# A recurrence of 1024 steps: bf16 splits of three gate products against float32 products with constant matmuls beside them

## The chip, the cores and the metric

The kernel runs as one program on 1 core of a Trainium2 chip. The metric is the device time of one execution in microseconds (us); lower is better. A core has five engines with instruction streams of their own: TensorE (PE in the rows, its weight loads PEld), VectorE (DVE), ScalarE (ACT), GpSimd (POOL) and SyncE (SP). [...] 

## The reference, cut to what matters

The program is a small network: six transformer layers, a gated recurrence over the sequence, six more layers, an expert layer, full attention and a second expert layer, with layer norms between. Only the recurrence is touched by the change. Its input is `x` with B = 2 rows of T = 1024 steps and 128 features; the state has 128 features.

```python
def step(carry, inp):
    h, c, n = carry
    xi_t, xf_t, xg_t, xo_t = inp            # x @ W*x + b, known ahead
    i_t = jax.nn.sigmoid(xi_t + h @ Wih)
    f_t = jax.nn.sigmoid(xf_t + h @ Wfh)
    g_t = jnp.tanh(xg_t + h @ Wgh)
    o_t = jax.nn.sigmoid(xo_t + h @ Woh)
    c_t = f_t * c + i_t * g_t
    n_t = f_t * n + i_t * jnp.exp(g_t @ Weg + beg)
    h_t = o_t * (c_t / n_t)
    return ((h_t, c_t, n_t), h_t)
```

Each step needs the `h` of the step before, so the 1024 steps are a chain.

## The kernel before, in words

Everything runs with features on the 128 partitions; a state is 128x2 (two rows of the batch). `recurrence_phase` (lines 952 to 1161) first loads the weights, splits those of the gates i, f and o into three bf16 parts each (lines 1004 to 1010), and then loops over 8 rounds (`Fori`, line 1078) of `ROUND` = 128 unrolled steps. A round is made of 8 chunks of `CH` = 16 steps; the chunks alternate between two sets of PSUM banks (`j`) and two buffers `hbuf`. The parts of a gate that don't depend on `h` (bias and `x @ W`) are put into the banks one chunk ahead by `project`, as 9 pieces: a float32 product of 32 columns after each odd step (line 1065), one more after step 0 (line 1067). The products with `h` are added on top of these.

The order of each engine is written out by hand, with a semaphore for each hand-over. In one step:

- TensorE (`tensor_steps`, lines 1048 to 1061): waits for `h_ready`; float32 product of gate g, which the compiler issues as two weight loads and two matmuls; then, from the three bf16 parts of `h` and of the weights, six small matmuls for each of i and f (a weight load each) and six for o; then it waits for `tg_ready` and does the float32 product with `Weg`; then a piece of `project` where one is due.
- ScalarE (lines 1089 to 1099): tanh of g, exp of -(i, f) together, exp of -o, exp of the `Weg` product.
- VectorE (lines 1109 to 1149): sigmoids from the exponentials, then the new denominator times (1 + e^-o) as `no`, the new numerator `cn[0]`, `rn = 1/no`, `h = cn[0] * rn` into `hbuf`; after that it makes the three bf16 parts of `h` (`hparts`, lines 1138 to 1143) and the new `cn[1]` (line 1146), off the way to `h`. A `scalar_tensor_tensor` whose scalar is a column per partition is issued once for each of the two batch rows.
- GpSimd adds `x` to a chunk of 16 `h` (line 1156) once that chunk is complete.

A wait that matters, in the code:

```python
                if n:
                    pe.wait_ge(h_ready, n)
                pe.matmul(g_bank[j][:, s * B:(s + 1) * B], Wg[:, 3, 1, :], h, start=False, stop=True,
                          skip_group_check=True).then_inc(g_done, 1)
```

The pieces of `project` and all else that follows on TensorE stand behind this wait in program order, and the next step's product stands behind them.

Of the kernel before, what the change touches and what calls it, by code (L numbers as in the profile page):

```python
# [933 lines left out]
GATES = ("i", "f", "o", "g")  # L941

EARLY_TERMS = [(0, 0), (1, 0), (2, 0), (0, 1), (1, 1)]
LAST_TERM = (0, 2)

MOST = 1e37


def recurrence_phase(nc, c):

    with ExitStack() as ctx:
        sb, ps, sem = scope(nc, ctx)  # L960
        Wg = sb("Wgates", [P, 4, 2, P])
        Wparts = sb("Wparts", [P, 3, 3, P], BF16)
        wrest = sb("wrest", [P, 3, P])
# [8 lines left out]
        g_bank = [ps(f"g_bank{i}", [P, 512]) for i in range(2)]
        s_bank = [ps(f"s_bank{i}", [P, 512]) for i in range(2)]
        o_bank = [ps(f"o_bank{i}", [P, 512]) for i in range(2)]
        e_bank = [ps(f"e_bank{i}", [P, 512]) for i in range(2)]
        w_in, zeroed, w_split, table_loaded = sem("r_w_in"), sem("r_zeroed"), sem("r_w_split"), sem("r_table_loaded")
        counted = [sem("r_" + x) for x in (
            "g_done", "s_done", "o_done", "e_done", "tg_ready", "es_ready", "ex_ready", "eo_ready", "h_ready",
            "h_first", "h_split", "rest_done", "so_done", "nso_done", "sg_done", "fno_done", "ig_done", "n_done", "no_done", "rn_done", "y_done")]
        (g_done, s_done, o_done, e_done, tg_ready, es_ready, ex_ready, eo_ready, h_ready,  # L980
         h_first, h_split, rest_done, so_done, nso_done, sg_done, fno_done, ig_done, n_done, no_done, rn_done, y_done) = counted

        with nc.Block() as block:
# [9 lines left out]
            @block.gpsimd  # L993
            def _(pool):
                pool.memset(cn[:, :, :], 0.0).then_inc(zeroed, 1)
                pool.memset(hbuf[1][:, :, :], 0.0).then_inc(zeroed, 1)
                pool.memset(hparts[:, :, :], 0.0).then_inc(zeroed, 1)

            @block.vector
            def _(dve):  # L1000

                dve.wait_ge(w_in, 16 * 10)
                W = Wg[:, 0:3, 1, :]
                dve.tensor_copy(Wparts[:, :, 0, :], W).then_inc(w_split, 1)
                dve.wait_ge(w_split, 1)
                dve.tensor_tensor(wrest[:, :, :], W, Wparts[:, :, 0, :], ALU.subtract).then_inc(w_split, 1)
                dve.wait_ge(w_split, 2)
                dve.tensor_copy(Wparts[:, :, 1, :], wrest[:, :, :]).then_inc(w_split, 1)
                dve.wait_ge(w_split, 3)
                dve.tensor_tensor(Wparts[:, :, 2, :], wrest[:, :, :], Wparts[:, :, 1, :], ALU.subtract).then_inc(w_split, 1)  # L1010

        def tensor_steps(pe, it, first_round):
            def project(j, at, which):


                gate, part = which // 2, which % 2
                if gate != 0 and gate != 1:
                    bank = {2: o_bank, 3: g_bank, 4: e_bank}[gate]
                    out = bank[j][:, 0:CH * B].rearrange("p (s b) -> p b s", b=B)
                    first = part == 0  # L1020
                else:
                    out = s_bank[j][:, 0:CH * 2 * B].rearrange("p (s g b) -> p g b s", g=2, b=B)[:, gate]
                    first = which == 0
                if part == 0:
                    lhsT, rhs = bias[0:1, gate, :], c.ones[0:1, 0:B * CH].rearrange("p (b s) -> p b s", b=B)
                else:
                    lhsT, rhs = Wg[:, gate, 0, :], c.xA[:, :, bass.ds(at, CH)]
                return pe.matmul(out, lhsT, rhs, start=first, stop=False, skip_group_check=True)

            def recur(out, gate, terms):  # L1030
                for w_part, h_part in terms:
                    last = pe.matmul(out, Wparts[:, gate, w_part, :], hparts[:, h_part, :], start=False,  # L1032
                                     stop=(w_part, h_part) == LAST_TERM, skip_group_check=True)
                return last
# [43 lines left out]
        with nc.Fori(0, T // ROUND) as it:  # L1078
            with nc.Block() as block:
# [5 lines left out]
                def _(act):  # L1085
                    for n in range(ROUND):
                        k, s = divmod(n, CH)
                        j = k % 2
                        act.wait_ge(g_done, n + 1)
                        act.activation(tg[:, :], g_bank[j][:, s * B:(s + 1) * B], ACT.Tanh).then_inc(tg_ready, 1)  # L1090
                        act.wait_ge(s_done, n + 1)
                        act.activation(es[:, :, :].rearrange("p g b -> p (g b)"), s_bank[j][:, s * 2 * B:(s + 1) * 2 * B],  # L1092
                                       ACT.Exp, scale=-1.0).then_inc(es_ready, 1)
                        act.wait_ge(o_done, n + 1)
                        act.activation(eo[:, :], o_bank[j][:, s * B:(s + 1) * B], ACT.Exp, scale=-1.0).then_inc(eo_ready, 1)
                        if n:
                            act.wait_ge(n_done, n)
                        act.wait_ge(e_done, n + 1)
                        act.activation(ex[:, :], e_bank[j][:, s * B:(s + 1) * B], ACT.Exp).then_inc(ex_ready, 1)

                @block.vector
                def _(dve):

                    for n in range(ROUND):
                        k, s = divmod(n, CH)
                        j = k % 2
                        if s == 0 and k >= 2:
                            dve.wait_ge(y_done, k - 1)
                        dve.wait_ge(es_ready, n + 1)
                        dve.tensor_scalar(sg[:, :, :], es[:, :, :], 1.0, None, ALU.add).then_inc(sg_done, 1)  # L1110
                        dve.wait_ge(eo_ready, n + 1)
                        dve.tensor_scalar(so[:, :], eo[:, :], MOST, 1.0, ALU.min, ALU.add).then_inc(so_done, 1)
                        dve.wait_ge(sg_done, 2 * n + 1)
                        dve.reciprocal(sg[:, :, :], sg[:, :, :]).then_inc(sg_done, 1)
                        dve.wait_ge(so_done, n + 1)
                        dve.tensor_tensor(nso[:, :], cn[:, 1, :], so[:, :], ALU.mult).then_inc(nso_done, 1)
                        dve.wait_ge(sg_done, 2 * n + 2)
                        dve.tensor_tensor(iso[:, :], sg[:, 0, :], so[:, :], ALU.mult)
                        dve.wait_ge(nso_done, n + 1)
# [499 lines left out]
```

## Time and profile before

| what | value |
|---|---|
| time, median of 3 runs | 7952.26 us |
| runs, lowest to highest | 7947.48 to 7956.73 us |
| span of the profiled execution, first to last instruction | 7947.7 us |
| stretch with the 1024 steps in it | 2336 to 5190 us of the span |
| mean granted TensorE clock over the span | 0.795 of full speed |

The span is the profiled execution itself; no other time is listed for it, and the three timed runs lie between 0.2 us below it and 9.0 us above it. The rows are read so: a row of the timeline gives the start, then the duration of the instructions on it from the first one's start to the last one's end (`x12` is 12 of them, which overlap), then in brackets the idle time of the engine before it and what ended that. [...]

### The profile page before, as it was taken

How to read it: one execution, taken by the hardware profiler on the slowest of the kernel's cores; microseconds unless marked ns; L12 is line 12 of the kernel's file. 1: busy time of each engine (PE TensorE's matmuls, PEld its weight loads, DVE VectorE, ACT ScalarE, POOL GpSimd, SP SyncE). 2: the span in 40 equal slices, each digit the busy share in tenths (PEclk: the TensorE clock that was granted, in tenths of full speed). 3: DMA queues.
4: the chain of work that ended last, by engine and by line, in shares of the span. 5: the costliest groups of instructions: out<-in, count | busy, mean ns of one | idle time of the engine just before them, and what ended most of it. 6: DMA issues, size and time to landing. Idle time of an engine off the chain costs nothing. (4 is left out here: it accounts for less than half of the span.)

```text
span 7947.7 us, 238408 instructions
## 1 busy us (share of the span) xinstructions
PE 6508.3 (82%) x89716; PEld 4710.8 (59%) x89716; DVE 5680.7 (71%) x26551; ACT 2813.2 (35%) x7328; POOL 1991.7 (25%) x2075
## 2 busy tenths in 40 slices
PE   8999999999976666666666666679999999999887
PEld 5656656565656565655656565656565655656544
DVE  6676767676767777777777777777666676767566
ACT  4444444444432222222222222234444444444311
POOL 4343535353510000000000000034444353535200
PEclk9999999999975555555555555589999999999898
DMA  0000000000000000000000000000000000000000
GB/s 28 11 4 14 1 14 1 14 1 14 1 15 2 2 2 2 2 2 2 2 2 2 2 2 2 2 4 0 15 11 4 11 4 14 1 14 1 18 2 12
DMA packets 30765, 50.49 MB, mean 6 GB/s; under 512 B 2032, under 2 KB 25291, under 8 KB 28235
## 3 DMA queue, kind: packets, MB, share of 16 engines
q1 hardware_dynamic: 29614, 40.54, 1.6%
q8 instruction: 425, 6.96, 0.4%
q14 instruction: 314, 2.56, 0.1%
q10 hardware_dynamic: 412, 0.42, 0.0%
HBM read 39.91 MB, written 1.05 MB: 5 GB/s over the span
## 5 line engine op out<-in xcount | busy, mean ns | idle before, releaser
L1048 PE MATMUL g_bank<-hbuf,Wgates 128*128 128x2 f32 x2048 | 600.9, 363 | 1024.2 <-DVE hbuf L1136 970.3
L1048 PEld LDWEIGHTS g_bank<-hbuf,Wgates 128*128 128x128 f32 x2048 | 513.0, 311 | 1140.0 <-DVE hbuf L1136 1085.3
L1090 ACT ACTIVATE tg<-g_bank 128x2 f32<-128x2 f32 x1024 | 176.1, 172 | 1690.9 <-PE g_bank L1048 1690.9
L1156 POOL TENSOR_TENSOR xB<-hbuf,xA 128x32 f32 x64 | 16.4, 256 | 2853.0 <-DVE hbuf L1136 2853.0
L371 POOL TENSOR_TENSOR t1b<-t1b,t2b 128x1024 f32<-128x1024 f32 x192 | 451.7, 2354 | 687.1 <-DVE t2b L523 687.1
L371 POOL TENSOR_TENSOR t1a<-t1a,t2a 128x1024 f32<-128x1024 f32 x192 | 451.7, 2354 | 684.7 <-DVE t2a L523 684.7
L1060 PE MATMUL e_bank<-tg,Weg 128*128 128x2 f32 x2048 | 579.4, 352 | 0.0
L1032 PEld LDWEIGHTS s_bank<-hparts,Wparts 128*128 128x128 bf16 x12288 | 571.0, 117 | 0.0
L1110 DVE TENSOR_SCALAR sg<-es 128x4 f32<-128x4 f32 x1024 | 174.4, 170 | 554.5 <-ACT es L1092 554.5
L1060 PEld LDWEIGHTS e_bank<-tg,Weg 128*128 128x128 f32 x2048 | 515.1, 312 | 0.0
L1032 PE MATMUL s_bank<-hparts,Wparts 128*128 128x2 bf16 x12288 | 469.6, 165 | 0.0
L555 DVE TENSOR_REDUCE ssqb<-sqb 128x16 f32<-128x1024 f32 x192 | 232.7, 1215 | 187.5 <-ACT sqb L634 187.5
L376 POOL TENSOR_TENSOR t1b<-t1b,rnormb 128x1024 f32<-128x1024 f32 x192 | 361.1, 1902 | 11.6 <-DVE rnormb L98 11.6
L376 POOL TENSOR_TENSOR t1a<-t1a,rnorma 128x1024 f32<-128x1024 f32 x192 | 361.0, 1901 | 11.6 <-DVE rnorma L98 11.6
L555 DVE TENSOR_REDUCE ssqa<-sqa 128x16 f32<-128x1024 f32 x192 | 232.5, 1215 | 182.3 <-ACT sqa L634 182.3
L1127 DVE SCALAR_TENSOR_TENSOR no<-ex,iso,fno 128x1 f32<-128x1 f32 x2048 | 352.0, 213 | 3.6 <-issue 1.7
L1146 DVE SCALAR_TENSOR_TENSOR cn<-ex,sg,fcn 128x1 f32<-128x1 f32 x2048 | 351.8, 214 | 0.0
L431 PEld LDWEIGHTS banksa<-KT,QTa 64*32 64x32 f32 x12288 | 292.1, 107 | 41.0 <-issue 41.0
L431 PEld LDWEIGHTS banksb<-KT,QTb 64*32 64x32 f32 x12288 | 292.1, 107 | 40.7 <-issue 40.7
L643 ACT COPY Vwb<-banksb 128x512 f32<-128x512 f32 x384 | 224.8, 586 | 256.5 <-PE banksb L475 256.1
L643 ACT COPY Vwa<-banksa 128x512 f32<-128x512 f32 x384 | 224.7, 586 | 255.9 <-PE banksa L475 255.5
L431 PE MATMUL banksa<-KT,QTa 64*32 64x64 f32 x12288 | 308.3, 218 | 0.0
(435 smaller groups left out, 16401.7 us busy)
## 6 DMA issues: line engine op xcount, KB each, us to landing
Wqkv<-in_L_ffn_Wqkv SPq DMA_DIRECT2D x13, 1536.0 KB, 6.5
Wo<-in_L_ffn_Wo SPq DMA_DIRECT2D x13, 512.0 KB, 7.6
W<-in_L_ffn_W SPq DMA_DIRECT2D x12, 341.0 KB
W<-in_L_ffn_W SPq DMA_DIRECT2D x12, 128.0 KB
xt<-in_L_attn_x SPq DMA_DIRECT2D x2, 512.0 KB
rope<-in_rope SPq DMA_DIRECT2D x1, 1024.0 KB, 7.5
out<-ot SPq DMA_DIRECT2D x4, 256.0 KB
W<-in_L_ffn_W SPq DMA_DIRECT2D x12, 42.5 KB
```

Of the source, the lines that this page charges most:

```text
L371: pool.tensor_tensor(t1[:, part], t1[:, part], t2[:, part], ALU.add).then_inc(s.rot_sum, 1)
L376: pool.tensor_tensor(qview(t1[:, part]), qview(t1[:, part]), c.rnorm[:, i * HEADS:(i + 1) * HEADS].unsqueeze(2).to_broadcast([P, HEADS, DH ...
L431: last = pe.matmul(sc[WIN * w:WIN * w + WIN, col:col + KEYS], c.QT[rows, pair, WIN * w:WIN * w + WIN], c.KT[b][rows, pair, WIN * w:WIN * w ...
L555: dve.tensor_reduce(c.ssq[:, i * HEADS:(i + 1) * HEADS], qview(sq[:, i * INNER:(i + 1) * INNER]), AX.X, ALU.add).then_inc(s.ssq_done, 1)
L643: act.copy(c.Vw[:, w, :], vo[:, bank * 512:(bank + 1) * 512]).then_inc(s.v_ready, 1)
L1032: last = pe.matmul(out, Wparts[:, gate, w_part, :], hparts[:, h_part, :], start=False, stop=(w_part, h_part) == LAST_TERM, skip_group_chec ...
L1048: pe.matmul(g_bank[j][:, s * B:(s + 1) * B], Wg[:, 3, 1, :], h, start=False, stop=True, skip_group_check=True).then_inc(g_done, 1)
L1060: pe.matmul(e_bank[j][:, s * B:(s + 1) * B], Weg[:, :], tg[:, :], start=False, stop=True, skip_group_check=True).then_inc(e_done, 1)
L1090: act.activation(tg[:, :], g_bank[j][:, s * B:(s + 1) * B], ACT.Tanh).then_inc(tg_ready, 1)
L1110: dve.tensor_scalar(sg[:, :, :], es[:, :, :], 1.0, None, ALU.add).then_inc(sg_done, 1)
L1127: last = dve.scalar_tensor_tensor(out=no[:, b:b + 1], in0=ex[:, b:b + 1], scalar=iso[:, b:b + 1], in1=fno[:, b:b + 1], op0=ALU.mult, op1=A ...
L1146: last = dve.scalar_tensor_tensor(out=cn[:, 1, b:b + 1], in0=ex[:, b:b + 1], scalar=sg[:, 0, b:b + 1], in1=fcn[:, 1, b:b + 1], op0=ALU.mul ...
```

## The change

All gate weights stay float32: the split of the weights, `hparts`, `hrest` and the four instructions that made them in each step go. The step on TensorE is now float32 products of i, g and f, the wait for the tanh, the `Weg` product, the float32 product of o, then `project` where due, and then `warm` = 4 matmuls after even steps and 3 after odd ones, with constant bf16 operands (the identity as weights, 512 columns of the mask), into a PSUM bank that nobody reads. ScalarE has five activations instead of four (i and f apart). VectorE keeps numerator and denominator over the common denominator f: `w = (1+e^-f)/(1+e^-i)`, `up = cn + w * (tanh g, exp)`, `h = up[0] / (up[1] * (1+e^-o))`, `cn = up / (1+e^-f)`. The order of the nine pieces of `project` and the placing of gates in banks change with it. Cut to its core (`...` marks what is left out):

```diff
-EARLY_TERMS = [(0, 0), (1, 0), (2, 0), (0, 1), (1, 1)]
-LAST_TERM = (0, 2)
-MOST = 1e37
+MOST = 1e30
-def recurrence_phase(nc, c):
+def recurrence_phase(nc, c, warm=4):
...
+        spare = ps("spare_bank", [P, 512])
...
-                dve.tensor_copy(Wparts[:, :, 0, :], W).then_inc(w_split, 1)
...
         def tensor_steps(pe, it, first_round):
+            pieces = [("e", 4, 0), ("i", 0, 0), ("i", 0, 1), ("f", 1, 0), ("f", 1, 1), ("o", 2, 0), ("o", 2, 1), ("g", 3, 0), ("g", 3, 1)]
...
+            def recur(gate, row, j, s, h):
+                return pe.matmul(columns(gate, j, s), Wg[:, row, 1, :], h, start=False, stop=True, skip_group_check=True)
...
                 if n:
                     pe.wait_ge(h_ready, n)
-                pe.matmul(g_bank[j][:, s * B:(s + 1) * B], Wg[:, 3, 1, :], h, start=False, stop=True,
-                          skip_group_check=True).then_inc(g_done, 1)
-                if n:
-                    pe.wait_ge(h_split, 2 * n - 1)
-                recur(i_out, 0, EARLY_TERMS)
-                recur(f_out, 1, EARLY_TERMS)
-                if n:
-                    pe.wait_ge(h_split, 2 * n)
-                recur(i_out, 0, [LAST_TERM])
-                recur(f_out, 1, [LAST_TERM]).then_inc(s_done, 1)
-                recur(o_out, 2, EARLY_TERMS + [LAST_TERM]).then_inc(o_done, 1)
+                recur("i", 0, j, s, h).then_inc(i_done, 1)
+                recur("g", 3, j, s, h).then_inc(g_done, 1)
+                recur("f", 1, j, s, h).then_inc(f_done, 1)
                 pe.wait_ge(tg_ready, n + 1)
-                pe.matmul(e_bank[j][:, s * B:(s + 1) * B], Weg[:, :], tg[:, :], start=False, stop=True,
-                          skip_group_check=True).then_inc(e_done, 1)
+                pe.matmul(columns("e", j, s), Weg[:, :], tg[:, :], start=False, stop=True, skip_group_check=True).then_inc(e_done, 1)
+                recur("o", 2, j, s, h).then_inc(o_done, 1)
+                if s == 0:
+                    project(1 - j, 0, 0)
                 if s % 2 == 1:
-                    project(1 - j, it * ROUND + (PAD + (k + 1) * CH), s // 2)
-                if s == 0:
-                    project(1 - j, 0, 8)
+                    project(1 - j, it * ROUND + (PAD + (k + 1) * CH), 1 + s // 2)
+                for _ in range(warm if s % 2 == 0 else max(warm - 1, 0)):
+                    pe.matmul(spare[:, :], c.identb[:, :], c.mask[:, :, :].rearrange("p t j -> p (t j)"), start=True, stop=True)
...
+                        act.wait_ge(i_done, n + 1)
+                        act.activation(ei[:, :], columns("i", j, s), ACT.Exp, scale=-1.0).then_inc(ei_ready, 1)
                         act.wait_ge(g_done, n + 1)
+                        act.activation(tg[:, :], columns("g", j, s), ACT.Tanh).then_inc(tg_ready, 1)
+                        act.wait_ge(f_done, n + 1)
+                        act.activation(ef[:, :], columns("f", j, s), ACT.Exp, scale=-1.0).then_inc(ef_ready, 1)
+                        act.wait_ge(e_done, n + 1)
+                        act.activation(ex[:, :], columns("e", j, s), ACT.Exp).then_inc(ex_ready, 1)
                         act.wait_ge(o_done, n + 1)
+                        act.activation(eo[:, :], columns("o", j, s), ACT.Exp, scale=-1.0).then_inc(eo_ready, 1)
...
+                        dve.wait_ge(ei_ready, n + 1)
+                        dve.tensor_scalar(di[:, :], ei[:, :], 1.0, None, ALU.add).then_inc(di_done, 1)
+                        dve.wait_ge(di_done, n + 1)
+                        dve.reciprocal(ri[:, :], di[:, :]).then_inc(ri_done, 1)
+                        dve.wait_ge(ef_ready, n + 1)
+                        dve.tensor_scalar(df[:, :], ef[:, :], MOST, 1.0, ALU.min, ALU.add).then_inc(df_done, 1)
+                        dve.wait_ge(ri_done, n + 1)
+                        dve.wait_ge(df_done, n + 1)
+                        dve.tensor_tensor(w[:, :], df[:, :], ri[:, :], ALU.mult).then_inc(w_done, 1)
+                        dve.reciprocal(rf[:, :], df[:, :]).then_inc(rf_done, 1)
+                        dve.wait_ge(w_done, n + 1)
+                        for b in range(B):
+                            last = dve.scalar_tensor_tensor(out=up[:, 0, b:b + 1], in0=tg[:, b:b + 1], scalar=w[:, b:b + 1],
+                                                            in1=cn[:, 0, b:b + 1], op0=ALU.mult, op1=ALU.add)
+                        last.then_inc(c_done, 1)
+                        dve.wait_ge(ex_ready, n + 1)
+                        for b in range(B):
+                            last = dve.scalar_tensor_tensor(out=up[:, 1, b:b + 1], in0=ex[:, b:b + 1], scalar=w[:, b:b + 1],
+                                                            in1=cn[:, 1, b:b + 1], op0=ALU.mult, op1=ALU.add)
+                        last.then_inc(n_done, 1)
+                        dve.wait_ge(eo_ready, n + 1)
+                        dve.wait_ge(n_done, n + 1)
+                        dve.scalar_tensor_tensor(out=mo[:, :], in0=eo[:, :], scalar=1.0, in1=up[:, 1, :],
+                                                 op0=ALU.add, op1=ALU.mult).then_inc(mo_done, 1)
+                        dve.wait_ge(mo_done, n + 1)
+                        dve.reciprocal(rm[:, :], mo[:, :]).then_inc(rm_done, 1)
...
+                        dve.wait_ge(rm_done, n + 1)
+                        dve.tensor_tensor(hbuf[j][:, :, s], up[:, 0, :], rm[:, :], ALU.mult).then_inc(h_ready, 1)
+                        dve.wait_ge(rf_done, n + 1)
+                        dve.tensor_tensor(cn[:, :, :], up[:, :, :], rf[:, :].unsqueeze(1).to_broadcast([P, 2, B]), ALU.mult).then_inc(state_done, 1)
+                        dve.wait_ge(state_done, n + 1)
```

## Rows read from the trace of the kernel before

**Rows 1.** The page: busy time by engine, and granted clock in 40 slices.

```profile
PE 6508.3 (82%) x89716; PEld 4710.8 (59%) x89716; DVE 5680.7 (71%) x26551; ACT 2813.2 (35%) x7328; POOL 1991.7 (25%) x2075
...
PEclk9999999999975555555555555589999999999898
```

**Rows 2.** Who waited for whom from 2336 to 5190: total us, times, longest.

```profile
PEld g_bank L1048 <- DVE hbuf L1136: 1085.3, 1016, 1.6
DVE sg L1110 <- ACT es L1092: 547.4, 1023, 7.7
PEld g_bank L1048 <- issue: 54.1, 7, 8.2
```

**Rows 3.** The timeline from 3000 to 3006, all engines: one step of it.

```profile
3000.83 0.16 DVE L1136 TENSOR_TENSOR hbuf<-cn,rn 128x2 f32<-128x2 f32 x1
...
3001.05 0.50 PEld L1048 LDWEIGHTS g_bank<-hbuf,Wgates 128*128 128x128 f32 x2 [0.83 <-DVE hbuf L1136]
3001.05 0.58 PE L1048 MATMUL g_bank<-hbuf,Wgates 128*128 128x2 f32 x2 [0.69 <-DVE hbuf L1136]
...
3001.49 0.46 PE L1032 MATMUL s_bank<-hparts,Wparts 128*128 128x2 bf16 x12
3001.67 0.17 ACT L1090 ACTIVATE tg<-g_bank 128x2 f32<-128x2 f32 x1 [1.61 <-PE g_bank L1048]
...
3001.95 0.50 PEld L1060 LDWEIGHTS e_bank<-tg,Weg 128*128 128x128 f32 x2
3001.97 0.57 PE L1060 MATMUL e_bank<-tg,Weg 128*128 128x2 f32 x2
3001.99 0.17 ACT L1092 ACTIVATE es<-s_bank 128x4 f32<-128x4 f32 x1
...
3002.27 0.17 DVE L1110 TENSOR_SCALAR sg<-es 128x4 f32<-128x4 f32 x1 [0.48 <-ACT es L1092]
...
3002.47 0.50 PEld L1028 LDWEIGHTS s_bank<-ones,gate_bias 1*128 1x128 f32 x2
3002.47 0.18 DVE L1114 RECIPROCAL sg<-sg 128x4 f32<-128x4 f32 x1
...
3002.97 0.34 DVE L1127 SCALAR_TENSOR_TENSOR no<-ex,iso,fno 128x1 f32<-128x1 f32 x2
3003.23 0.16 DVE L1131 TENSOR_TENSOR cn<-ig,fcn 128x2 f32<-128x2 f32 x1
3003.35 0.17 DVE L1133 RECIPROCAL rn<-no 128x2 f32<-128x2 f32 x1
3003.55 0.16 DVE L1136 TENSOR_TENSOR hbuf<-cn,rn 128x2 f32<-128x2 f32 x1
...
3003.77 0.50 PEld L1048 LDWEIGHTS g_bank<-hbuf,Wgates 128*128 128x128 f32 x2 [0.80 <-DVE hbuf L1136]
```

**Rows 4.** The timeline: weight loads of an expert's 512-column float32 matmuls.

```profile
7549.98 0.33 PEld L1312 LDWEIGHTS ezmoe<-Wemoe,ext0moe 128*128 128x128 f32 x1 [0.52 <-issue]
7550.83 0.33 PEld L1312 LDWEIGHTS ezmoe<-Wemoe,ext0moe 128*128 128x128 f32 x1 [0.52 <-issue]
```

**Rows 5.** Busy time by stretch: from:to, us, engines, PEclk, DMA share, GB/s.

```profile
2312.50:2319.30 6.80, 4.46 (x16) 2.86 (x16) 4.91 (x16) 2.35 (x4) 0.00 (x0) 0.50 0.00 0
2327.70:2333.30 5.60, 5.11 (x18) 4.48 (x18) 0.00 (x0) 1.49 (x2) 0.00 (x0) 0.50 0.00 0
2336.00:5190.00 2854.00, 1829.23 (x23656) 1708.35 (x23656) 2193.18 (x19444) 692.29 (x4092) 16.38 (x64) 0.50 0.01 2
7548.96:7551.68 2.72, 2.72 (x3) 1.17 (x4) 0.53 (x3) 0.00 (x0) 0.18 (x1) 0.50 0.00 0
7552.20:7555.60 3.40, 3.40 (x9) 1.52 (x8) 3.24 (x14) 0.00 (x0) 0.29 (x1) 1.00 0.03 7
7807.90:7811.30 3.40, 3.08 (x12) 2.15 (x12) 2.50 (x8) 1.64 (x3) 0.00 (x0) 0.50 0.00 0
```

**Rows 6.** Groups of 7528.6 to 7530.9: 20-column float32 matmuls at clock 1.00.

```profile
L1214 PE MATMUL elmoe<-wg2moe,hTmoe 32*128 32x20 f32 x20 | 2.4, 262 | 0.0
```

More of the change, by code:

```diff
@@ L972, in recurrence_phase @@
[L972 to L976, printed above, removed]
+        tg, ei, ef, eo, ex = sb("tg", [P, B]), sb("ei", [P, B]), sb("ef", [P, B]), sb("eo", [P, B]), sb("ex", [P, B])
+        di, ri, df, rf, w = sb("di", [P, B]), sb("ri", [P, B]), sb("df", [P, B]), sb("rf", [P, B]), sb("w", [P, B])
@@ L977, in recurrence_phase @@
+        cn, up = sb("cn", [P, 2, B]), sb("up", [P, 2, B])
+        mo, rm = sb("mo", [P, B]), sb("rm", [P, B])
+        io_bank = [ps(f"io_bank{i}", [P, 512]) for i in range(2)]
+        ge_bank = [ps(f"ge_bank{i}", [P, 512]) for i in range(2)]
+        f_bank = [ps(f"f_bank{i}", [P, 512]) for i in range(2)]
+        spare = ps("spare_bank", [P, 512])
+        w_in, zeroed, table_loaded = sem("r_w_in"), sem("r_zeroed"), sem("r_table_loaded")
         counted = [sem("r_" + x) for x in (
-            "g_done", "s_done", "o_done", "e_done", "tg_ready", "es_ready", "ex_ready", "eo_ready", "h_ready",
@@ L983, in recurrence_phase @@
+        (i_done, g_done, f_done, e_done, o_done, ei_ready, tg_ready, ef_ready, ex_ready, eo_ready,
+         h_ready, di_done, ri_done, df_done, w_done, c_done, n_done, mo_done, rm_done, rf_done, state_done, y_done) = counted
         with nc.Block() as block:
@@ L996, in _, with columns @@
                 pool.memset(hbuf[1][:, :, :], 0.0).then_inc(zeroed, 1)
[L997 to L1003, printed above, removed]
-                dve.tensor_copy(Wparts[:, :, 0, :], W).then_inc(w_split, 1)
[L1005 to L1010, printed above, removed]
+        def columns(gate, j, s, width=1):
+            bank, at = {"i": (io_bank, 0), "o": (io_bank, 1), "g": (ge_bank, 0), "e": (ge_bank, 1), "f": (f_bank, 0)}[gate]
+            at = (at * CH + s) * B
+            return bank[j][:, at:at + width * B]
@@ L1012, in tensor_steps @@
         def tensor_steps(pe, it, first_round):
+            pieces = [("e", 4, 0), ("i", 0, 0), ("i", 0, 1), ("f", 1, 0), ("f", 1, 1), ("o", 2, 0), ("o", 2, 1), ("g", 3, 0), ("g", 3, 1)]
             def project(j, at, which):
[L1016 to L1020, printed above, removed]
-                else:
-                    out = s_bank[j][:, 0:CH * 2 * B].rearrange("p (s g b) -> p g b s", g=2, b=B)[:, gate]
-                    first = which == 0
@@ L1024, in project @@
[L1024 to L1034, printed above, removed]
+                gate, row, part = pieces[which]
@@ new lines, in project @@
+                out = columns(gate, j, 0, CH).rearrange("p (s b) -> p b s", b=B)
+                if part == 0:
+                    lhsT, rhs = bias[0:1, row, :], c.ones[0:1, 0:B * CH].rearrange("p (b s) -> p b s", b=B)
+                else:
+                    lhsT, rhs = Wg[:, row, 0, :], c.xA[:, :, bass.ds(at, CH)]
+                return pe.matmul(out, lhsT, rhs, start=(gate in ("e", "i", "f") and part == 0), stop=False, skip_group_check=True)
+            def recur(gate, row, j, s, h):
+                return pe.matmul(columns(gate, j, s), Wg[:, row, 1, :], h, start=False, stop=True, skip_group_check=True)
@@ L1111, in _ @@
[L1111 to L1117, printed above, removed]
@@ L1125, in _ @@
-                        dve.wait_ge(ex_ready, n + 1)
-                        for b in range(B):
-                            last = dve.scalar_tensor_tensor(out=no[:, b:b + 1], in0=ex[:, b:b + 1], scalar=iso[:, b:b + 1],
-                                                            in1=fno[:, b:b + 1], op0=ALU.mult, op1=ALU.add)
-                        last.then_inc(no_done, 1)
-                        dve.wait_ge(ig_done, n + 1)
-                        dve.tensor_tensor(cn[:, 0, :], ig[:, :], fcn[:, 0, :], ALU.add)
@@ L1132, in _ @@
-                        dve.wait_ge(no_done, n + 1)
-                        dve.reciprocal(rn[:, :], no[:, :]).then_inc(rn_done, 1)
-                        dve.wait_ge(rn_done, n + 1)
-                        h = hbuf[j][:, :, s]
-                        dve.tensor_tensor(h, cn[:, 0, :], rn[:, :], ALU.mult).then_inc(h_ready, 1)
-                        dve.tensor_tensor(hparts[:, 0, :], cn[:, 0, :], rn[:, :], ALU.mult).then_inc(h_first, 1)
-                        dve.wait_ge(h_first, n + 1)
@@ L1140, in _ @@
-                        dve.tensor_tensor(hparts[:, 1, :], h, hparts[:, 0, :], ALU.subtract).then_inc(h_split, 1)
-                        dve.tensor_tensor(hrest[:, :], h, hparts[:, 0, :], ALU.subtract).then_inc(rest_done, 1)
-                        dve.wait_ge(rest_done, n + 1)
-                        dve.tensor_tensor(hparts[:, 2, :], hrest[:, :], hparts[:, 1, :], ALU.subtract).then_inc(h_split, 1)
-                        for b in range(B):
-                            last = dve.scalar_tensor_tensor(out=cn[:, 1, b:b + 1], in0=ex[:, b:b + 1], scalar=sg[:, 0, b:b + 1],
-                                                            in1=fcn[:, 1, b:b + 1], op0=ALU.mult, op1=ALU.add)
@@ L1148, in _ @@
-                        last.then_inc(n_done, 1)
-                        dve.wait_ge(n_done, n + 1)
+                        dve.wait_ge(c_done, n + 1)
+                        dve.wait_ge(rm_done, n + 1)
+                        dve.tensor_tensor(hbuf[j][:, :, s], up[:, 0, :], rm[:, :], ALU.mult).then_inc(h_ready, 1)
+                        dve.wait_ge(rf_done, n + 1)
+                        dve.tensor_tensor(cn[:, :, :], up[:, :, :], rf[:, :].unsqueeze(1).to_broadcast([P, 2, B]), ALU.mult).then_inc(state_done, 1)
```

31 lines of the change are left out of this document (2 added, 29 removed).

## The prediction

> **What bounds the kernel now.** I read the page first: TensorE is busy 82% of the span, but its granted clock is at half for the whole middle of it, 2336 to 5190 [rows 1]. In that stretch no engine is full: TensorE 1829 of 2854 us, VectorE 2193 [rows 5]. That is the picture of a chain, and the waits say which: TensorE waits 1085 us for `h`, VectorE 547 us for the exponentials [rows 2]. The timeline of a step then gives the chain piece by piece. From `h` to `h` (3000.83 to 3003.55) it takes 2.72 us [rows 3]: 0.22 to the first weight load; 0.58 for the float32 product of g; 18 small bf16 matmuls from 3001.49 to 3001.97, 0.027 each; the exponential at 3001.99; 0.28 to VectorE; 1.28 there until `h` is written again. 1024 steps at 2.72 are 2785 us of the 2854; the other 69 (0.07 a step) are mostly the starts of the 8 rounds (TensorE "issue" 54 us in 7 pieces [rows 2]). I keep the 69.
>
> So the change is worth 1024 times what it does to a step. The sum is made against the span of the profiled execution, 7947.7 us; the median of the runs is 4.6 us above, and I put the result on the median.
>
> [...] Removed: 18 bf16 matmuls, 0.48 us. Added: float32 products of i, f and o. A float32 product costs two weight loads. Where the next weights can be loaded behind it, the next matmul starts 0.44 after it (g at 3001.05, first bf16 matmul at 3001.49); from the `Weg` product to the next product's load it is 0.52 (3001.95 to 3002.47) [rows 3]. i, g, f, e and o follow each other like the first case, so 5 x 0.445 = 2.23; bound 5 x 0.52 = 2.60. Does e wait for the tanh? g ends at 0.445 + 0.58 = 1.03; the tanh starts 0.04 later, takes 0.17, and TensorE answers 0.05 after: 1.29, before f gives up its place at 1.34. No stall. `project` is 9 products in 16 steps, of 0.5: 0.28 a step.
>
> The constant matmuls are 3.5 a step, 512 columns each. Their form in bf16 isn't timed here at this clock; the nearest rows are the expert's float32 matmuls, 0.85 us from one weight load to the next at 7550 [rows 4] (clock 0.50 there [rows 5]), which at the full clock are 8 loads in 3.40 us, 0.425 each [rows 5]. [...] 3.5 x 0.43 = 1.50. One thing comes back: the first weight load of the next step's i hides under the last constant matmul, -0.21.
>
> Sum: 2.23 + 0.28 + 1.50 - 0.21 = **3.80 us of TensorE per step**; bound above 4.2 (products at 0.52, constant ones at 0.45), below 3.70.
>
> [...] Times from the first load of i, dependent VectorE instructions 0.20 apart (3002.27 to 3002.47, 3003.35 to 3003.55), a pair of `scalar_tensor_tensor` 0.26 until the next instruction and 0.38 until one that needs it (3002.97 to 3003.35) [rows 3]. f ends at 0.89 + 0.58 = 1.47; exp 1.51 to 1.68; `df` 1.79; `w` 1.99; first pair 2.19; second pair 2.45 (exp of e at 1.96 to 2.13, in time); `mo` 2.83; `rm` 3.04; `h` 3.24; next load 3.46. The o path (o ends 2.36, exp until 2.57) isn't last. So 3.46 of chain against 3.80 of TensorE: the constant matmuls are **not** in a gap, they stand in front of the next i and set the step. Without them it would already be slower than 2.72, as three products at half clock take 1.3 where 18 small matmuls took 0.48. That `w` and the pair over the common denominator come only after f, and `hparts` falls away, is inside this sum; the `hparts` instructions were off the path already (the load of g doesn't wait for them). What goes before the loop (four conversions) happens once. GpSimd's addition follows `h` as before and covers itself. ACT has 5 x 0.17 = 0.85 of work in 3.8. None of these adds to the sum.
>
> **Total at 1.2 GHz:** 1024 x 3.82 (0.02 for hand-over) = 3912, plus 69 = 3981 for the stage against 2854: +1127. 7947.7 + 1127 = 9075, with the 4.6 of the median 9079; I say **9075 us**. Bounds: step 3.70: 8957; step 4.2: 9469.
>
> **Which clock.** All hangs on this. The stage is entered at 0.50 and the rows show what TensorE did without a rise: 64% busy with small products for 2854 us; 91% busy (5.11 of 5.60) with float32 products of 32 columns at 2327.7; 16 transposes of 128 columns in 6.80 us (their columns pass for 16 x 0.213 = 3.4 us, half the time) at 2312.5; even 12 of them in 3.40 us at 7807.9, also at 0.50 [rows 5]. The rise shown is after 512-column matmuls stood end to end for 2.7 us (7548.96 to 7551.68, then 1.00) [rows 5]. In a step of 3.8 us at half clock the constant matmuls pass columns for 1.5 us in one block, 1.3 or 1.7 us long, 39% of the time; between blocks stand products of 2 columns, the kind that never raised anything. This resembles the stretch at 2312.5 and not the one at 7549. So I take 0.50 throughout.
>
> [...]
>
> **Rivals.**
>
> 1. *The full clock comes and holds.* A product of few columns then costs 20 instructions in 2.3 us, 0.115 x 2 = 0.23, and ends 0.115 + 0.26 = 0.38 after its first load [rows 6]. i 0, g 0.23, f 0.46, ending 0.38, 0.61, 0.84. ScalarE: exp i, tanh 0.65 to 0.82, exp f 0.88 to 1.05. `df` 1.16, `w` 1.36, pairs 1.56 and 1.82, `mo` 2.20, `rm` 2.41, `h` 2.61, load 2.83. TensorE needs 5 x 0.23 + 0.14 + 3.5 x 0.215 = 2.04 and is hidden. Step 2.82 against 2.72: +102 us, **8055**. Even then VectorE's longer tail has eaten the faster products. [...] Against it: the stretches above, and that such a step leaves TensorE waiting 0.8 us with narrow work beside.
> 2. *The other side: full clock and a shorter tail.* Place: f to `w` to the two pairs. If the o path ended last, not this one, `mo` would start at 1.82 (o ends 0.88 + 0.23 + 0.38 = 1.49, exp to 1.71) and the step take 2.45; halfway is 2.6: 1024 x -0.12 = -123, **7829**. It decides in the kernel's favour as soon as the step is under 2.72. Against it: it needs both the clock and dependent instructions closer than 0.20 everywhere, which no row shows.
> 3. *The clock changes back and forth*, some steps at 3.8, some at 2.8: **8100 to 8950**. For it: blocks of wide columns sometimes lie near each other. Against it: at half clock each is followed by 2.0 us of narrow products, so nothing starts the first rise.
> 4. *The constant matmuls are left out or cost nothing*: the chain alone, 3.46: 7952 + 1024 x 0.74 = **8710**. Nothing in the diff lets them go; the bank is written and never read, but they are instructions.
>
> **How the numbers follow.** Forecast 0.80, its own range 8955 to 9430, as 9469 needs every product at 0.52. Rival 1 0.07, rival 2 0.05, its neighbour within 0.2% of no change 0.01, rivals 3 and 4 together 0.07. The forecast's own range holds about 0.77 (what it misses lies mostly just below, where products overlap more); down to 8700 come rival 4 and a part of 3: 0.80. So the range is 8700 to 9430. 0.2%, some 16 us, is about what a measurement of this kernel can tell from no change. Faster 0.06, same 0.02, slower 0.92.
>
> **What would show it.** Right: granted clock 0.50 over the whole recurrence, which is 3.9 to 4.1 ms long; TensorE over 95% busy in it; waits of TensorE for `h` almost gone; constant matmuls 0.43 apart; the row of `h` 3.8 us apart; VectorE idle over 1 us a step. Wrong: PEclk of 1.00 anywhere inside the stage (rivals 1 to 3); steps of 2.8 with `h` as TensorE's releaser (1); steps of 3.8 whose i waits for `h` (then my chain is too short, not my TensorE too long); products 0.52 apart would put it at 9.3 to 9.4 ms.

## The result and the profile after

| | before | after |
|---|---|---|
| median | 7949.87 us | 8999.45 us |
| ratio after/before, 95% interval | | 1.1315 (1.1297 to 1.1333) |
| span of the profiled execution | 7947.7 us | 8997.6 us |
| mean granted clock of the span | 0.795 | 0.76 |
| first `h` to last `h` | 2853.0 us | 3895.0 us |

One of the four runs of the changed kernel took 12406 us with a mean clock of 0.52; it is left out of the ratio (without it the median is 8999.32 us), and nothing below rests on it.

The kernel is 1050 us slower, 1042 of them between the first and the last `h`. The page of the kernel after, to be read against [rows 1] (PEclk is the granted clock, the share of its full speed that TensorE's clock had, here in tenths):

```profile
PE 8529.1 (95%) x81012; PEld 5970.6 (66%) x81012; DVE 5402.8 (60%) x20403; ACT 3000.2 (33%) x8352; POOL 1990.8 (22%) x2074
...
PEclk9999999999655555555555555555999999999988
```

TensorE went from 82% to 95% busy with fewer instructions, and the clock's valley is as deep as before and wider. Two stretches of it, against [rows 5]; the columns are those of that group:

```profile
2341.00:6233.00 3892.00, 3849.37 (x14951) 2965.37 (x14952) 1916.58 (x13294) 879.22 (x5112) 15.26 (x63) 0.50 0.00 1
4000.00:4100.00 100.00, 100.00 (x391) 77.13 (x392) 50.19 (x348) 23.22 (x135) 0.24 (x1) 0.50 0.00 1
```

TensorE is busy for 3849 of 3892 us, 100 of 100 in the middle, and its granted clock stays at 0.50. Who waited for whom in this stretch, against [rows 2]:

```profile
DVE di L1058 <- ACT ei L1041: 1143.4, 1022, 7.6
...
DVE df L1062 <- ACT ef L1045: 416.9, 1014, 0.5
PEld io_bank L995 <- DVE hbuf L1087: 384.2, 952, 0.8
...
PE io_bank L995 <- issue: 42.6, 7, 6.3
```

Before, both TensorE (1085 us) and VectorE (547 us) waited. Now TensorE's matmuls wait for `h` nowhere; a weight load does for 384 us, behind a constant matmul that is still running. VectorE waits 1143 + 417 us. One step of the kernel after, one without a piece of `project`, against [rows 3] (the first row is from the step before):

```profile
3999.83 0.56 PE L995 MATMUL ge_bank<-hbuf,Wgates 128*128 128x2 f32 x2
...
4002.71 0.16 DVE L1087 TENSOR_TENSOR hbuf<-up,rm 128x2 f32<-128x2 f32 x1
...
4002.99 0.76 PEld L995 LDWEIGHTS io_bank<-hbuf,Wgates 128*128 128x128 f32 x2 [0.28 <-DVE hbuf L1087]
4003.42 0.43 PE L995 MATMUL io_bank<-hbuf,Wgates 128*128 128x2 f32 x2
...
4003.71 0.56 PE L995 MATMUL ge_bank<-hbuf,Wgates 128*128 128x2 f32 x2
...
4004.13 0.57 PE L995 MATMUL f_bank<-hbuf,Wgates 128*128 128x2 f32 x2
...
4004.56 0.57 PE L1011 MATMUL ge_bank<-tg,Weg 128*128 128x2 f32 x2
...
4004.94 0.17 DVE L1062 TENSOR_SCALAR df<-ef 128x2 f32<-128x2 f32 x1 [0.41 <-ACT ef L1045]
4004.99 0.56 PE L995 MATMUL io_bank<-hbuf,Wgates 128*128 128x2 f32 x2
...
4005.21 0.16 DVE L1065 TENSOR_TENSOR w<-df,ri 128x2 f32<-128x2 f32 x1
...
4005.41 1.87 PE L1018 MATMUL spare_bank<-mask,identb 128*128 128x512 bf16 x4
...
4006.13 0.16 DVE L1079 SCALAR_TENSOR_TENSOR mo<-eo,up 128x2 f32<-128x2 f32 x1
...
4006.33 0.17 DVE L1082 RECIPROCAL rm<-mo 128x2 f32<-128x2 f32 x1
4006.60 0.16 DVE L1087 TENSOR_TENSOR hbuf<-up,rm 128x2 f32<-128x2 f32 x1
...
4006.82 0.59 PEld L995 LDWEIGHTS io_bank<-hbuf,Wgates 128*128 128x128 f32 x2 [0.44 <-DVE hbuf L1087]
4007.07 0.42 PE L995 MATMUL io_bank<-hbuf,Wgates 128*128 128x2 f32 x2
```

This is a queue and not a chain. From i to the next i, 3.65 us: 0.29 for i (its first weight load is hidden), then 0.42, 0.43, 0.43, 0.42 for the other four products, then four constant matmuls until 4007.07, 0.415 each. `h` has been there since 4006.76. The step before has a piece of `project` and one constant matmul less, and takes 3.88 (its g product at 3999.83, this one's at 4003.71). The chain through VectorE is close behind: without the constant matmuls a step takes 3.55 us (`e1_none` below), 0.10 less than this one.

### The profile page after: what moved, and what is told of

It is laid out like the page before. It is cut to its first block and busy times, and to the rows that moved or that the text cites. A ratio compares the mean times of both kernels' runs of the same rounds, so it can differ in the third digit from the quotient of the medians.

```text
span 8997.6 us, 216915 instructions
## 1 busy us (share of the span) xinstructions
PE 8529.1 (95%) x81012; PEld 5970.6 (66%) x81012; DVE 5402.8 (60%) x20403; ACT 3000.2 (33%) x8352; POOL 1990.8 (22%) x2074
## 5 line engine op out<-in xcount | busy, mean ns | idle before, releaser
L1018 PE MATMUL spare_bank<-mask,identb 128*128 128x512 bf16 x3584 | 1706.9, 624 | 0.0
L995 PEld LDWEIGHTS io_bank<-hbuf,Wgates 128*128 128x128 f32 x4096 | 1196.2, 326 | 478.8 <-DVE hbuf L1087 384.2
L995 PE MATMUL io_bank<-hbuf,Wgates 128*128 128x2 f32 x4096 | 1021.1, 319 | 43.2 <-issue 42.6
L1018 PEld LDWEIGHTS spare_bank<-mask,identb 128*128 128x128 bf16 x3584 | 503.6, 164 | 444.2 <-issue 423.7
L995 PE MATMUL ge_bank<-hbuf,Wgates 128*128 128x2 f32 x2048 | 579.5, 353 | 0.0
L1011 PE MATMUL ge_bank<-tg,Weg 128*128 128x2 f32 x2048 | 579.5, 353 | 0.0
L995 PE MATMUL f_bank<-hbuf,Wgates 128*128 128x2 f32 x2048 | 579.5, 353 | 0.0
L995 PEld LDWEIGHTS ge_bank<-hbuf,Wgates 128*128 128x128 f32 x2048 | 559.7, 333 | 0.0
L995 PEld LDWEIGHTS f_bank<-hbuf,Wgates 128*128 128x128 f32 x2048 | 559.7, 333 | 0.0
L1011 PEld LDWEIGHTS ge_bank<-tg,Weg 128*128 128x128 f32 x2048 | 517.9, 313 | 0.0
```

The costliest lines, as they stand in the source:

```text
L995: return pe.matmul(columns(gate, j, s), Wg[:, row, 1, :], h, start=False, stop=True, skip_group_check=True)
L1011: pe.matmul(columns("e", j, s), Weg[:, :], tg[:, :], start=False, stop=True, skip_group_check=True).then_inc(e_done, 1)
L1018: pe.matmul(spare[:, :], c.identb[:, :], c.mask[:, :, :].rearrange("p t j -> p (t j)"), start=True, stop=True)
```

## The experiments

Each run stands beside runs of the kernel before on the same chip, medians of which were 7947 to 7953 us.

### Four runs that take the change apart

`e1_none` is the changed kernel without the constant matmuls (first diff), `e2_eight` with twice as many (`warm=8` in the same line), `e3_burst` keeps its 4 and puts a burst of 20 ahead of each round (second diff), and `e4_update` puts the new update alone into the kernel before (third diff: TensorE, ScalarE and the parts of `h` stay as before).

```diff
-def recurrence_phase(nc, c, warm=4):
+def recurrence_phase(nc, c, warm=0):
```

```diff
+            for _ in range(20):
+                pe.matmul(spare[:, :], c.identb[:, :], c.mask[:, :, :].rearrange("p t j -> p (t j)"), start=True, stop=True)
             for n in range(ROUND):
```

```diff
+                        dve.tensor_scalar(di[:, :], es[:, 0, :], 1.0, None, ALU.add).then_inc(di_done, 1)
+                        dve.tensor_scalar(df[:, :], es[:, 1, :], MOST, 1.0, ALU.min, ALU.add).then_inc(df_done, 1)
...
-                        dve.tensor_scalar(sg[:, :, :], es[:, :, :], 1.0, None, ALU.add).then_inc(sg_done, 1)
...
-                        dve.tensor_tensor(h, cn[:, 0, :], rn[:, :], ALU.mult).then_inc(h_ready, 1)
...
+                        dve.tensor_tensor(h, up[:, 0, :], rm[:, :], ALU.mult).then_inc(h_ready, 1)
```

> The changed kernel with no constant matmuls (warm = 0), all else the same. Theory 1 (TensorE's own work sets the step, the constant matmuls stand in front of the next i product): what is left is the chain i, g, f, exp of f, df, w, two pairs, mo, rm, h. With the distances of the changed kernel's trace (mo to rm 0.19, rm to h 0.27, h to the next load 0.22) a step is 3.4 to 3.55 us instead of 3.74: total 8700 to 8830 us, clock still 0.50. Theory 2 (the chain through VectorE is already last and the constant matmuls are hidden): about 9000 us. Theory 3 (they do help the clock somewhere): over 9000 us.

> The changed kernel with 8 constant matmuls after even steps and 7 after odd ones. Theory 1 (the clock rises when wide matmuls fill enough of what TensorE does; 4 a step were too few): the block of 3.4 us at half clock lifts it, PEclk 1.00 in the recurrence, a float32 product then takes 0.22, a constant matmul 0.215, and TensorE's sum 1.1 + 0.14 + 1.6 meets the chain of about 2.8: step 2.8 to 3.0, total 8050 to 8250 us. Theory 2 (nothing with narrow products between the blocks lifts it): step 2.0 + 0.3 + 7.5 x 0.43 - 0.2 = 5.3 us, total 10500 to 10700 us, PEclk 0.50.

> The changed kernel with 20 extra constant matmuls back to back at the start of each of the 8 rounds (8.5 us at half clock, about 6 with the rise in it), which should lift the clock once a round. Theory 1 (4 a step neither lift nor hold it): PEclk 1.00 for some us after each burst, then 0.50 again; total 9010 to 9070 us. Theory 2 (4 a step are enough to hold a clock that is up, they only could not raise it): PEclk 1.00 through the round, step about 2.85, total 8050 to 8200 us.

> The kernel before with its bf16 products, and only VectorE's update over the common denominator taken from the change. Theory 1 (the longer tail on VectorE is a cost of its own, hidden in the changed kernel by TensorE): from the exponentials at 0.94 the chain di, ri, w, two pairs, mo, rm, h ends 3.1 to 3.3 us after the load of g instead of 2.72: total 8300 to 8550 us. Theory 2 (all of the loss is the float32 products and the constant matmuls): 7950 us, within 20.

| run | median | ratio to before (95%) |
|---|---|---|
| e1_none | 8796.45 us | 1.1065 (1.1046 to 1.1083) |
| e2_eight | 8291.58 us | 1.0427 (1.0409 to 1.0444) |
| e3_burst | 9026.17 us | 1.1352 (1.1333 to 1.1371) |
| e4_update | 8476.05 us | 1.0659 (1.0641 to 1.0677) |

All four went the way of the first theory, three of them inside its range. `e2_eight` has the full clock that it said, but at 8292 us lies 42 above its 8050 to 8250: a step with a bias piece of `project` takes 3.16 us there and one without a piece 2.95. **e1_none:** the constant matmuls cost 203 us (8999 to 8796). Waits of that run, from 2340 to 6038:

```profile
PEld io_bank L995 <- DVE hbuf L1087: 1115.4, 1016, 1.7
PE io_bank L995 <- DVE hbuf L1087: 1000.8, 1016, 1.6
```

TensorE waits for `h` again, its matmul too and not only the weight load: without them the step is a chain, 3.55 us, and still slower than before.

**e2_eight and e3_burst:** stretches of both; the first row is e2_eight, whole stage:

```profile
2340.00:5523.00 3183.00, 3099.77 (x19055) 2107.93 (x19054) 1915.65 (x13296) 881.21 (x5115) 15.21 (x63) 0.99 0.01 1
```

and this is e3_burst, the burst of the first round and the rest of the round:

```profile
2336.70:2343.50 6.80, 6.55 (x39) 4.41 (x38) 3.16 (x22) 1.72 (x10) 0.00 (x0) 1.00 0.00 0
2343.60:2828.30 484.70, 478.80 (x1854) 366.51 (x1853) 236.69 (x1642) 108.47 (x630) 1.93 (x8) 0.50 0.00 1
```

Twice as many constant matmuls make the kernel 708 us **faster** than four, because the clock goes from 0.50 to 0.99. There a float32 product takes 0.22 (the g product starts at 4002.82, that of f at 4003.04) and a constant matmul 0.215 (eight from 4003.91 to 4005.63), against 0.43 and 0.415 at 0.50. A burst with four behind it lifts the clock for 6.8 us, and four a step neither raise nor hold it. So four a step have the whole price and none of the use.

**e4_update:** the update over the common denominator costs 523 us (8476 against the 7953 of its own runs of the kernel before) where TensorE isn't in its way, half of the change's loss. A part of its step:

```profile
4000.44 0.50 PEld L1048 LDWEIGHTS g_bank<-hbuf,Wgates 128*128 128x128 f32 x2 [1.82 <-DVE hbuf L1137]
...
4001.75 0.17 DVE L1108 TENSOR_SCALAR di<-es 128x2 f32<-128x2 f32 x1 [0.51 <-ACT es L1092]
...
4003.27 0.17 DVE L1131 RECIPROCAL rm<-mo 128x2 f32<-128x2 f32 x1
4003.54 0.17 DVE L1137 TENSOR_TENSOR hbuf<-up,rm 128x2 f32<-128x2 f32 x1
```

From the first VectorE instruction to `h` it takes 1.79 us; before, it was 1.28 [rows 3]. The old update started the denominator's f part from the old state while the exponential of e was on its way; the new one has two pairs, a product and a reciprocal, each after the other. Not all of it is arithmetic: `mo` and `h` each have two waits here, which cost 0.07 apiece (see the section on two waits; `rm` to `h` is 0.27 in these rows), so an estimate of 2 x 0.07 x 1024 = 143 of the 523 us is the order of the waits. This version wasn't run with them exchanged.

With e1_none and e4_update the loss is split: update 523, the rest of the new step 320 more (8476 to 8796: float32 products for the bf16 ones, their order, and i and f apart on ScalarE, which no run separates), constant matmuls 203 more (8796 to 8999). The order of taking them matters, since a queue hides a chain.

### How many hold the clock, and whether the kernel before can use it

`e5_six` is the changed kernel with 6 after even and 5 after odd steps. The `f` runs put constant matmuls into the kernel before; the banks of g and e become one, so that there is one to spare (this alone wasn't run). The diff is that of `f2_b66burst` against the kernel before.

```diff
-        g_bank = [ps(f"g_bank{i}", [P, 512]) for i in range(2)]
+        g_bank = [ps(f"ge_bank{i}", [P, 512]) for i in range(2)]
+        spare = ps("spare_bank", [P, 512])
...
-        e_bank = [ps(f"e_bank{i}", [P, 512]) for i in range(2)]
+        e_bank = [g_bank[i][:, CH * B:2 * CH * B] for i in range(2)]
...
-                    first = part == 0
+                    first = part == 0 and gate != 3
...
-                for which in range(9):
+                for which in [8, 0, 1, 2, 3, 4, 5, 6, 7]:
...
+            for _ in range(12):
+                pe.matmul(spare[:, :], c.identb[:, :], c.mask[:, :, :].rearrange("p t j -> p (t j)"), start=True, stop=True)
             for n in range(ROUND):
...
                     project(1 - j, 0, 8)
+                for _ in range(6 if s % 2 == 0 else 6):
+                    pe.matmul(spare[:, :], c.identb[:, :], c.mask[:, :, :].rearrange("p t j -> p (t j)"), start=True, stop=True)
```

`f1_b87` has 8 and 7 and no burst, `f3_b76` 7 and 6 and no burst, `f4_b55burst` 5 and 5 with the burst. `f5_a66burst` is the changed kernel with 6 and 6 and the burst.

> The changed kernel with 6 constant matmuls after even steps and 5 after odd ones, between 4 (clock 0.50 throughout) and 8 (clock 0.99, step 3.06, TensorE full). If the clock rises by itself (theory 1a), TensorE has room at full clock and the chain alone sets the step, 2.8 to 2.95 us with VectorE's tail: total 8100 to 8200 us, faster than with 8. If it doesn't (theory 1b), the step is 2.0 + 0.28 + 5.5 x 0.43 - 0.2 = 4.4 us at half clock: total 9600 to 9800 us, slower than with 4. Nothing between.

> The kernel before (bf16 products, its own update) with 8 constant matmuls after even and 7 after odd steps; the banks of g and e are made one to have room for the spare one. Theory 1 (the constant matmuls buy clock, and the loss of the change is its products and its update): PEclk 1.00; the chain saves 0.2 on the g product and up to 0.15 on the bf16 ones, step 2.45 to 2.65 us, TensorE nearly full: total 7700 to 7880 us, faster than before. Theory 2 (the chain before waits for VectorE's parts of h and ACT, the clock buys nothing): total 7950 us or, with TensorE overfull, up to 8100 us.

> As f1_b87, with 6 constant matmuls after every step and 12 back to back at the start of each round. If 6 a step hold the clock that the burst raised: TensorE has 0.3 us of room, the chain sets the step at 2.45 to 2.6 us, total 7680 to 7850 us, less than f1_b87. If they don't hold it: step 0.45 + 0.48 + 0.5 + 0.28 + 2.6 - 0.2 = 4.1 us at half clock, total 9300 to 9400 us.

> As f1_b87, with 7 after even and 6 after odd steps and no burst. If these raise and hold the clock: total 7680 to 7850 us, between f1_b87 and f2_b66burst or level with the better one. If the clock falls and rises by turns: 8000 to 9000 us.

> The kernel before with 5 constant matmuls after every step and the burst of 12 at the start of each round (6 of them gave 7807 us). If 5 hold the clock: TensorE has more room and the chain is the same 2.56 us, total 7790 to 7820 us. If they hold it only some of the time: the clock goes back and forth, a step at half clock is about 3.7 us, total between 8000 and 9000 us. Theory: with 6 and 5 the changed kernel went back and forth 219 times, so a smaller number must be near its edge here too, though a shorter step packs the wide matmuls closer; I lean to the second.

> The changed kernel with 6 constant matmuls after every step, odd ones too, and the burst of 12 at the start of each round: does its own design work once the clock is held? If held: TensorE needs 1.1 + 0.15 + 1.3 = 2.6 us, so the chain sets the step, 2.83 us after rival 1 of the prediction, 2.85 to 2.95 by the distances of the changed kernel's trace (rm to h 0.27): total 8080 to 8200 us, slower than before even at full clock. If VectorE's tail were shorter than I worked out: under 7950 us. If the clock isn't held: 9000 to 9800 us.

| run | median | ratio to before (95%) | granted clock of the stage |
|---|---|---|---|
| e5_six | 9509.08 us | 1.197 (1.1951 to 1.1988) | 0.59 |
| f1_b87 | 7880.89 us | 0.9916 (0.9903 to 0.993) | 0.98 |
| f2_b66burst | 7807.3 us | 0.9821 (0.9808 to 0.9835) | 0.99 |
| f3_b76 | 7832.01 us | 0.9851 (0.9836 to 0.9866) | 0.98 |
| f4_b55burst | 8825.8 us | 1.1099 (1.1081 to 1.1118) | 0.51 |
| f5_a66burst | 8247.04 us | 1.0383 (1.0365 to 1.04) | 0.98 |

**e5_six** is a miss in kind: I had written "nothing between", and it is between. The clock went up 219 times in the stage. Its whole stage and two stretches inside:

```profile
2339.00:6706.00 4367.00, 4219.04 (x16666) 2945.10 (x17008) 1917.03 (x13301) 879.93 (x5115) 15.22 (x63) 0.59 0.00 1
3000.00:3100.00 100.00, 98.14 (x375) 69.37 (x381) 42.77 (x297) 19.78 (x115) 0.48 (x2) 0.55 0.00 1
3200.00:3300.00 100.00, 97.20 (x405) 66.53 (x413) 46.68 (x323) 21.11 (x123) 0.48 (x2) 0.64 0.00 1
```

It is slower than with 4 and slower than with 8: between the two lies a hill, not a slope. **f4_b55burst** is on the same hill from the other side: 5 a step don't hold, in the stage of the kernel before, what the burst raised, and 6 do (`f2_b66burst`). Two more missed their ranges: `f1_b87` by 1 us and `f5_a66burst` by 47, both above.

**f1_b87, f2_b66burst, f3_b76** are faster than both kernels, clear of the noise but by less than 2% of the kernel before. The best is f2_b66burst, 1.8% below it: its whole stage and a step:

```profile
2340.00:5040.00 2700.00, 2529.80 (x29242) 1671.79 (x29756) 2182.58 (x19358) 679.81 (x4076) 16.13 (x63) 0.99 0.01 2
```

```profile
4000.90 0.16 DVE L1141 TENSOR_TENSOR hbuf<-cn,rn 128x2 f32<-128x2 f32 x1
...
4001.12 0.38 PE L1051 MATMUL ge_bank<-hbuf,Wgates 128*128 128x2 f32 x2
...
4001.39 0.47 PE L1033 MATMUL s_bank<-hparts,Wparts 128*128 128x2 bf16 x12
...
4003.46 0.16 DVE L1141 TENSOR_TENSOR hbuf<-cn,rn 128x2 f32<-128x2 f32 x1
```

The step is 2.56 instead of 2.72. The g product ends 0.38 instead of 0.58 after its start, and the bf16 matmuls follow 0.27 instead of 0.44 behind that start; the twelve of i and f take as long as before (0.47 against 0.46), so only 0.16 is won. With 8 and 7 TensorE is too full for the steps that have a bias piece of `project` (2.74 us); with 7 and 6 the clock comes up later in a round (7 to 31 us at half clock between two rounds, where f2_b66burst has 7 to 10).

**f5_a66burst** shows what the change's own design gives at full clock: 2.95 us a step where it holds, 4% slower than before. The clock rises 14 times in its 8 rounds, so inside most rounds it fell once.

### Two waits in front of one instruction

In the trace after, an instruction that depends on the one before it starts 0.20 later (`mo` to `rm`, 4006.13 to 4006.33), but `w` starts 0.27 after `df` and `h` 0.27 after `rm`. These have two waits, and so has `mo`. Ahead of each of the three the trace shows a semaphore instruction of 0.02 us under the line of the wait written last, which is the late one here, 1024 times (L1064 ahead of `w`, L1078 ahead of `mo`, L1086 ahead of `h`); under the line of the wait written first (L1063, L1077, L1085) it shows none. The one on L1064 starts 0.21 after `df` here and 0.01 after it in `g1_none_swap`. That the other wait belongs to the instruction itself is my reading. `g1_none_swap` and `g2_a66_swap` only exchange the two lines at the three places:

```diff
-                        dve.wait_ge(c_done, n + 1)
                         dve.wait_ge(rm_done, n + 1)
+                        dve.wait_ge(c_done, n + 1)
                         dve.tensor_tensor(hbuf[j][:, :, s], up[:, 0, :], rm[:, :], ALU.mult).then_inc(h_ready, 1)
```

> e1_none (no constant matmuls, chain-bound at 3.55 us a step, 8796 us) with the two waits in front of each of w, mo and h written in the other order, so that the semaphore that comes last stands on the instruction itself and the one that came long before in the separate wait. Theory (the 0.26 to 0.27 us from df to w and from rm to h, against 0.20 elsewhere, is that separate wait instruction on the late semaphore): 3 x 0.07 = 0.2 us a step goes, 1024 x 0.2 = 205: total 8570 to 8620 us. Rival (the 0.07 are something else, such as the operand that another instruction wrote): 8790 to 8800 us.

> f5_a66burst (the changed kernel with its clock held at full, 2.95 us a step, 8247 us) with the same three pairs of waits in the other order. Theory: the chain falls to 2.75 us, TensorE needs about 2.6, total 8020 to 8080 us; still above the kernel before, as two pairs, mo and rm all come after f. Rival: 8230 to 8260 us.

g1_none_swap: 8561.15 us, 1.077 (1.0752 to 1.0788), 235 less than e1_none and 9 below its range. g2_a66_swap: 8045.38 us, 1.0123 (1.0106 to 1.014), 202 less than f5_a66burst. The rows of g1_none_swap:

```profile
3999.82 0.50 PEld L995 LDWEIGHTS io_bank<-hbuf,Wgates 128*128 128x128 f32 x2 [1.13 <-DVE hbuf L1087]
...
4001.30 0.17 ACT L1045 ACTIVATE ef<-f_bank 128x2 f32<-128x2 f32 x1 [0.26 <-PE f_bank L995]
...
4001.51 0.17 DVE L1062 TENSOR_SCALAR df<-ef 128x2 f32<-128x2 f32 x1 [0.41 <-ACT ef L1045]
4001.71 0.16 DVE L1065 TENSOR_TENSOR w<-df,ri 128x2 f32<-128x2 f32 x1
...
4002.17 0.34 DVE L1074 SCALAR_TENSOR_TENSOR up<-ex,w,cn 128x1 f32<-128x1 f32 x2
4002.55 0.16 DVE L1079 SCALAR_TENSOR_TENSOR mo<-eo,up 128x2 f32<-128x2 f32 x1
4002.74 0.17 DVE L1082 RECIPROCAL rm<-mo 128x2 f32<-128x2 f32 x1
4002.94 0.16 DVE L1087 TENSOR_TENSOR hbuf<-up,rm 128x2 f32<-128x2 f32 x1
```

`df` to `w` and `rm` to `h` are now 0.20, the pair to `mo` 0.38 instead of 0.45 (4005.68 to 4006.13 in the kernel after). Three times 0.07, 1024 times: 215 us, for an exchange of lines. The kernel after itself, where TensorE sets the step, wasn't run with it.

The kernel before has such a place too, and there it is on the chain. `sg` waits for `n_done`, written at the end of the step before, and then for `es_ready`, which is the late one; it starts 0.28 after `es` (3001.99 to 3002.27 [rows 3]), while `df`, which has one wait, starts 0.21 after `ef` in the rows above. By these rows an exchange there is worth about 0.07 a step, some 70 us; this is an estimate, and no run tried it.

## Why the prediction was right

**The bound.** Before: a chain of 1024 steps at half clock; the changes lie in it alone: 1042 of the 1050 us.

**The clock,** on which all hung. Forecast 0.50 throughout; it is 0.50. For 4 a step this is shown from both sides: they don't raise the clock (0.50 for 3892 us) and don't hold one that is up (e3_burst, 0.50 right after the burst). The 1.2 GHz in the forecast stands for this 0.50; no run shows a clock in GHz. The reason given, that a block of wide matmuls followed by narrow products is like the stretches that raised nothing, holds for this number alone: e2_eight has the same narrow products between blocks twice as long, and 0.99. Its list of stretches wasn't whole either. In the trace of the kernel before, 16 transposes of 128 columns stand end to end for 3.65 us from 5193.0, 0.23 each at 0.50, and the clock is 1.00 for 3.4 us from 5196.7, so matmuls of 512 columns were not the only ones seen to raise it. The forecast judged by likeness and had no measure of how near the edge it was; two more matmuls a step (e5_six) already raise the clock 219 times. That TensorE is nearly always busy didn't decide it: it was so for 3849 of 3892 us and had 0.50.

**TensorE sets the step, not the chain.** Right, shown by the waits and by e1_none, 203 us less without the constant matmuls. The distance was smaller than forecast: 3.46 against 3.80, 0.34 a step, and measured 3.55 against 3.76, 0.21.

**The size,** 80 us too high: the sum was 9079, rounded to a forecast of 9075, and measured was 8999. Four terms were too big. The hand-over of 0.02 that I added isn't there, and the constant matmuls take 0.415 each and not 0.43, 0.05 a step: together 0.07, 72 us. No run shows a constant matmul of 0.43, nor the 0.40 and 0.45 of its bounds. The 0.43 was my estimate, half of the expert's 0.85 [rows 4], and the bounds were guesses around it; the runs show 0.415 at a clock of 0.50 and, for rival 1's 0.215, 0.215 at full clock (`e2_eight`). The five products with the hidden load, 2.23 - 0.21 = 2.02, took 1.99 (4003.42 to 4005.41), as a product was 0.43 and not 0.445 but the hidden load gave back 0.14 and not 0.21: about 25 us. The remainder over 1024 steps, put at 69 us, was about 45, as I had taken the short steps' 2.72 for the mean of all, which is 2.74 inside a round. Against these 121 us stand two. `project` costs 0.31 a step and not 0.28 (a step takes 3.65 us without a piece, 3.68 with an `x @ W` piece in place of one constant matmul and 3.88 with a bias piece): about 27 us. And 8 us lie outside the stage. That accounts for 86 where the sum was 80 off.

**The chain without them,** forecast 3.46, measured 3.55. Two errors nearly cancel. A price was missing, 0.07 for each of three double waits. With these gone g1_none_swap is at 3.34, so the rest of my chain was 0.12 too long. Most of that is the way to `df`: its exponential starts 1.48 after the load of i (forecast 1.51), but `df` starts 0.21 behind that and not 0.28. I had read the 0.28 from `es` to `sg`, without seeing that a double wait is in it.

**Rival 1,** the full clock with a tail of VectorE that eats it, was put at 8055 us: f5_a66burst, which has that clock, is at 8247, and without its double waits at 8045. **Rival 2,** faster than before at full clock, needed dependent instructions clearly closer than 0.20; the rows show 0.19 at the least (`mo` to `rm` in g1_none_swap), and the changed design was slower than before in all eight versions of it that ran. **Rival 3,** a clock that changes back and forth, isn't this kernel, but it is e5_six, at 9509 above the range of 8100 to 8950, and for a few us of each round f4_b55burst, at 8826 inside it. **Rival 4,** constant matmuls at no cost, was put at 8710; e1_none, where they are really gone, is at 8796.

## What to carry to other kernels

Constant matmuls that shall lift TensorE's clock are no filler to be added by feel: measure the granted clock of the stage for each number of them, and go on past the first failures, since 4, 6 and 8 a step gave 8999, 9509 and 8292 us. Before buying clock, ask how much of the chain gets shorter by it: here 0.16 of 2.72 us, as in f2_b66burst VectorE (1.29 us from `sg` to `h`, 1.28 before), ScalarE (0.17 an activation in both), the semaphores (0.22 from `h` to the next load in both) and even the small bf16 matmuls (0.47 against 0.46) took as long as before. And where an instruction has two waits, write the one that comes last first, and look in the trace for distances of 0.27 where others have 0.20.

## What was not expected

- A busy TensorE doesn't mean a fast one: 100 of 100 us busy at 0.50, for 3.9 ms.
- The order of two `wait_ge` lines is worth 0.07 us on VectorE; at three places that was 202 and 235 us in two versions.
- Between too few constant matmuls and enough there is a version worse than either (e5_six, 219 rises of the clock), so that a search that stops at the first worse number doesn't find the one that works.
- At full clock the 12 bf16 matmuls with weight loads of their own took 0.47 us, no less than the 0.46 at half clock. What limits them there wasn't tried; in this step their last ones also wait for the third part of `h`.
